# A Mamba-style cross-attention block: two bursts of ScalarE work split, three more GpSimd products, fillers in the head

## The reference

```python
# per batch of 4; DI = 512 channels, N = 16 states, 512 positions
xin = in_proj(ctx)                              # 256 -> 512
u   = silu(causal_conv4(xin) + conv_b)
dt_low, B, C = split(x_proj(u))                 # 16, 16, 16 rows
dt  = softplus(dt_proj(dt_low) + dt_b)
state = state * exp(dt * A) + (dt * u) * B      # along the positions, 16 states a channel
y   = sum_n(state * C) + D * u
y   = y * silu(layernorm(x).T)                  # the gate
x   = x + y.T
out = x + layernorm(x) @ sum_r(factors[r]) / sqrt(8) + bias
```

## Time and profile before

| | us |
|---|---|
| median of 3 runs | 483.63 (482.84 to 483.75) |
| the profiled execution's own time | 482.48 |
| its span | 480.7 |
| VectorE busy | 453.5 (94%) |
| TensorE busy | 432.1 (90%) |
| GpSimd busy | 420.6 (88%) |
| ScalarE busy | 344.7 (72%) |

### The profile page before, as it was taken

The page is one execution under the profiler, slowest core; times in us unless marked ns, Lnnn a source line. Parts: engine busy times, 40 slices in busy tenths (PEclk is TensorE's granted clock), DMA queues, the critical chain, the costliest instruction groups (busy, mean ns, idle before and its releaser), DMA issues.

```text
span 480.7 us, 4118 instructions
## 1 busy us (share of the span) xinstructions
PE 432.1 (90%) x1119; PEld 185.3 (39%) x1119; DVE 453.5 (94%) x327; ACT 344.7 (72%) x578; POOL 420.6 (88%) x223
## 2 busy tenths in 40 slices
PE   8799797999979868898989789899979999989996
PEld 5134343434434233333434244343434343344432
DVE  5797999989999999989999999999999899999996
ACT  4669574977659788796869977697879876654422
POOL 4369999998979899997999979797998958999972
PEclk9989999999999989999999999999999999999999
DMA  5799746438982000100694000000396000000002
GB/s 193 267 355 350 200 80 138 83 55 217 292 337 88 1 0 0 42 25 1 191 412 168 0 22 1 0 24 0 132 381 237 1 22 23 22 22 22 0 1 88
DMA packets 16847, 53.96 MB, mean 112 GB/s; under 512 B 1828, under 2 KB 2084, under 8 KB 15800
## 3 DMA queue, kind: packets, MB, share of 16 engines
q1 hardware_dynamic: 15384, 45.14, 25.9%
q0 software_dynamic: 1152, 8.39, 8.8%
q10 hardware_dynamic: 288, 0.18, 0.1%
HBM read 49.24 MB, written 4.46 MB: 112 GB/s over the span
## 4 chain that ended last, share of the span: by engine, by line
POOL 53%; issue 20%; DVE 11%; ACT 6%; PE 4%; DMA 4%; SPq 1%; POOLq 0%; DVEq 0%; ACTq 0%
POOL h L1093 40%; POOL h L1086 9%; DVE dA L946 7%; POOL dtu L1079 3%; DMA c_rep<-bc_scratch 2%; PE y L519 2%; DVE acc L920 2%; ACT dA L776 1%; DMA chan<-channel 1%; DVE h L952 1%; PE work L415 1%; POOL fsum L1123 1%; DVE h L946 1%; ACT gate L690 0%; SPq L331 0%
## 5 line engine op out<-in xcount | busy, mean ns | idle before, releaser
L1093 POOL TENSOR_TENSOR h<-b_rep,dtu 128x1024 f32<-128x1024 f32 x127 | 302.3, 2446 | 12.3 <-DMA b_rep<-bc_scratch 11.3
L519 PE MATMUL y<-h,ident 128*128 128x512 f32 x508 | 236.5, 602 | 34.9 <-DVE h L952 33.0
L946 DVE TENSOR_TENSOR_SCAN dA<-dA,h 128x1024 f32<-128x1024 f32 x97 | 221.8, 2287 | 11.6 <-ACT dA L776 11.1
L776 ACT ACTIVATE dA<-dt,a_neg 128x512 f32<-128x512 f32 x256 | 166.0, 681 | 92.9 <-DVE h L952 76.2
L519 PEld LDWEIGHTS y<-h,ident 128*128 128x128 f32 x508 | 92.8, 190 | 166.2 <-issue 103.7
L952 DVE TENSOR_TENSOR h<-dA,c_rep 128x1024 f32<-128x1024 f32 x96 | 117.1, 1220 | 2.4 <-DMA c_rep<-bc_scratch 0.3
L1086 POOL TENSOR_TENSOR h<-h,c_rep 128x1024 f32<-128x1024 f32 x31 | 74.5, 2403 | 22.3 <-DVE h L946 22.3
L946 DVE TENSOR_TENSOR_SCAN h<-dA,h 128x1024 f32<-128x1024 f32 x31 | 70.6, 2279 | 0.1
L403 PE MATMUL work<-ctx_sb,w_in 128*128 128x512 f32 x60 | 30.6, 644 | 0.3 <-DMA w_in<-w_inT 0.2
L507 PE MATMUL work<-fsum,xnT 128*128 128x512 f32 x64 | 28.8, 592 | 0.0
L920 DVE SCALAR_TENSOR_TENSOR acc<-work,chan,acc 128x511 f32<-128x511 f32 (+2 forms) x30 | 21.6, 731 | 1.3 <-ACT acc L655 1.2
(11 more groups left out here) (128 smaller groups left out, 375.3 us busy)
## 6 DMA issues: line engine op xcount, KB each, us to landing
b_rep<-bc_scratch SPq DMA_DIRECT2D x32, 512.0 KB, 9.7
c_rep<-bc_scratch SPq DMA_DIRECT2D x32, 512.0 KB, 9.3
fsum<-factors POOLq DMA_DIRECT2D x8, 1024.0 KB, 8.3
x<-x SPq DMA_DIRECT2D x4, 1024.0 KB, 7.7
out<-x SPq DMA_DIRECT2D x16, 256.0 KB, 2.0
ctx_sb<-ctxT SPq DMA_DIRECT2D x3, 512.0 KB, 5.7
ctx_sb<-ctxT SPq DMA_DIRECT2D x2, 256.0 KB, 4.4
w_in<-w_inT SPq DMA_DIRECT2D x1, 384.0 KB, 5.2
```

Source lines behind the costliest of these rows:

```text
L519: mm = pe.matmul(y[:], ident[:], h[:, (s * PAIRS + j) % H_RING, i, :], start=False, stop=(j == sum_order(s)[-1] and i == 1))
L776: act.activation(dA[:, j % 2, i, :], dt[:, k % 2, :], ACT.Exp, scale=a_neg[:, k, 2 * j + i:2 * j + i + 1]).then_inc(exp_done, 1)
L946: dve.tensor_tensor_scan(pair if on_pool(s * PAIRS + j) else decay, decay, pair, 0.0, ALU.mult, ALU.add).then_inc(scanned, 1)
L1093: pool.tensor_tensor(h[:, (s * PAIRS + j) % H_RING], b_rep[:, j], dtu[:, k % 2, :].unsqueeze(1).to_broadcast([P, 2, L]), ALU.mult).then_in ...
```

## The change

- `SOFTPLUS_SLOTS`: softplus goes from slot 2 to slot 0 in steps 4, 8 and 12.
- The gate burst is made in two halves of two blocks each, each with its own table loads: slots 4 and 6 in step 0, slots 2 and 5 in steps 4, 8 and 12. The first half waits for one gate product fewer.
- The silu burst is made in two parts: blocks 0 to 2 of the next batch in slot 4 where k is 1 (steps 1, 5, 9), block 3 in slot 4 where k is 2 (steps 2, 6, 10).
- `STATS_SLOTS`: the statistics are in slot 5 in steps 0 and 2, in slot 3 in all others.
- `POOL_C`: steps 3, 9 and 11 have one C product more on GpSimd (pair 2 in step 3, pair 4 in steps 9 and 11). With it the order of TensorE's sums changes in these steps.
- `FIRST_FILL`: 6, 0, 2 and 2 zero-weight matmuls of 128 x 512 (bf16) ahead of the four parts of the first `x_proj`, and 3 behind it, into a bank of dA that is not yet used.

```diff
--- before.py
+++ after.py
@@ -57,11 +57,14 @@
 TENSOR_CONV = (5, 6, 7, 8, 9)
 SUM_ORDERS = {(0,): (1, 0, 2, 3, 4, 5, 6, 7), (0, 2): (1, 0, 3, 2, 4, 5, 6, 7), (0, 2, 4): (1, 0, 3, 2, 5, 4, 6, 7),
               (0, 4): (1, 0, 2, 3, 5, 4, 6, 7)}
-POOL_C = ((0, 4), (0,), (0, 2), (0,), (0, 2), (0, 2), (0, 2), (0, 2, 4), (0, 2), (0, 2), (0, 2), (0, 2), (0, 2), (0, 2),
-          (0, 2), (0, 2))
-SOFTPLUS_SLOT = 2
+POOL_C = ((0, 4), (0,), (0, 2), (0, 2), (0, 2), (0, 2), (0, 2), (0, 2, 4), (0, 2), (0, 2, 4), (0, 2), (0, 2, 4), (0, 2),
+          (0, 2), (0, 2), (0, 2))
+SOFTPLUS_SLOTS = (2, 2, 2, 2, 0, 2, 2, 2, 0, 2, 2, 2, 0, 2, 2, 2)
+GATE_SLOTS = ((4, 6), (2, 5), (2, 5), (2, 5))
 C_LAG = 3
+STATS_SLOTS = (5, 3, 5, 3, 3, 3, 3, 3, 3, 3, 3, 3, 3, 3, 3, 3)
 TENSOR_RESIDUAL = (0, 1, 2, 6, 8)
+FIRST_FILL = (6, 0, 2, 2, 3)
 IDLE_FILL = {(0, -1): 14, (0, 3): 3, (1, 3): 4, (3, 3): 4, (4, 1): 3, (5, 6): 2, (7, 6): 2, (8, 1): 2, (8, 6): 2, (9, 6): 2,
              (10, 1): 4, (11, 1): 2, (12, 1): 3, (13, 1): 3, (14, 3): 3}
 
@@ -416,9 +419,15 @@
                                    stop=(i == TAPS - 1))
                 mm.then_inc(conv_mm, 1)
 
+            def fill_first(i):
+
+                for _ in range(FIRST_FILL[i]):
+                    pe.matmul(dA[:, 1, 1, :], still[:], ones[:], start=True, stop=True)
+
             def x_proj(b):
                 for k in range(KB):
                     if b == 0:
+                        fill_first(k)
                         pe.wait_ge(u_done, k + 1)
                     mm = pe.matmul(first_bc if b == 0 else work2[0:2 * N + BC_ROW, :], w_x[:, k, :], u[:, b % 2, k, :], start=(k == 0),
                                    stop=(k == KB - 1))
@@ -614,6 +623,7 @@
             pe.wait_ge(w_x_landed, 16)
             pe.wait_ge(pads_ready, 1)
             x_proj(0)
+            fill_first(KB)
             pe.wait_ge(w_dt_landed, 16)
             pe.wait_ge(conv, conv_count(KB - 1))
             pe.wait_ge(dtl_evac, 1)
@@ -673,20 +683,20 @@
                 act.wait_ge(conv, conv_count(k))
                 act.activation(u[:, 0, k, :], acc[:, k, :], ACT.Silu).then_inc(u_done, 1)
 
-            def silu_batch(b):
-
-                wait_conv(act, b * KB + KB - 1)
+            def silu_blocks(b, first, last):
+
+                wait_conv(act, b * KB + last - 1)
                 if b >= 2:
                     act.wait_ge(y_init, (b - 1) * KB)
                     act.wait_ge(d_dtu, (b - 1) * KB)
-                act.activation(u[:, b % 2], acc[:], ACT.Silu).then_inc(u_done, KB)
-
-            def gate_batch(b):
+                act.activation(u[:, b % 2, first:last], acc[:, first:last], ACT.Silu).then_inc(u_done, last - first)
+
+            def gate_half(b, half):
 
                 act.wait_ge(g_nb, (b + 1) * KB)
                 if b > 0:
-                    act.wait_ge(gated, b * KB)
-                for k in range(KB):
+                    act.wait_ge(gated, b * KB - 1 + half)
+                for k in range(half * (KB // 2), (half + 1) * (KB // 2)):
                     act.activation(gate[:, k, :], x1_block(b, k), ACT.Silu, bias=g_r[:, 2, k:k + 1],
                                    scale=g_r[:, 1, k:k + 1]).then_inc(g_done, 1)
 
@@ -801,7 +811,7 @@
                         act.wait_ge(f_centred, i + 1)
                         act.activation(fsum[:, i, :], fsum[:, i, :], ACT.Copy, scale=FR ** -0.5).then_inc(f_scaled, 1)
 
-                    if j == SOFTPLUS_SLOT and is_d:
+                    if j == SOFTPLUS_SLOTS[s] and is_d:
                         act.preload_act_table_set("softplus")
                         softplus(s + 1)
                         act.preload_act_table_set("natural_log_exp_and_others")
@@ -823,21 +833,21 @@
                         conv_out(KB + 1)
                     if j == 3 and s > 0 and s + KB + 1 in TENSOR_CONV:
                         conv_out(s + KB + 1)
-                    if j == (5 if k == 0 else 3) and is_g:
+                    if j == STATS_SLOTS[s] and is_g:
                         act.wait_ge(x_landed, (b + 2) * 16)
                         act.wait_ge(g_nb, (b + 1) * KB)
                         minus_mean(g_mv, b + 1, k, g_scratch, g_mean)
                     if j == 3 and s - 1 in TENSOR_RESIDUAL:
                         x1_evac(s - 1)
-                    if j == 4 and k == 0:
+                    if k == 0 and j in GATE_SLOTS[b]:
                         act.preload_act_table_set("silu_and_others")
-                        gate_batch(b)
+                        gate_half(b, GATE_SLOTS[b].index(j))
                         act.preload_act_table_set("natural_log_exp_and_others")
-                    if j == 4 and k == KB - 2 and b + 1 < BATCH:
+                    if j == 4 and k in (1, KB - 2) and b + 1 < BATCH:
                         act.preload_act_table_set("silu_and_others")
-                        silu_batch(b + 1)
+                        silu_blocks(b + 1, *((0, KB - 1) if k == 1 else (KB - 1, KB)))
                         act.preload_act_table_set("natural_log_exp_and_others")
-                    if j == (5 if k == 0 else 3) and is_g:
+                    if j == STATS_SLOTS[s] and is_g:
                         var_sum(g_mv, b + 1, k, g_scratch, g_mean, s + 1, g_var)
                     if j in (2 if s == STEPS - 1 else 4 if s == STEPS - 2 else 6 if s == STEPS - 3 else 5, 7):
                         for w in w_at(s)[j // 7:j // 7 + 1]:
```

## The result

| | before | changed |
|---|---|---|
| median, us | 483.63 (5 runs) | 480.31 (479.59 to 481.48, 5 runs) |
| ratio | | 0.9934 [0.9919, 0.9948] |
| the profiled execution, us | 482.48 | 481.48 |

What follows compares the result with a forecast made beforehand. Outside head and tail, VectorE's work plus ten waits for ScalarE's decay factors (11.1 us) bound the kernel. Step terms summed to -2.5, or -2.8 with some 0.1 more per removed wait: 483.63 to 480.8 us, range 478.5 to 483.8.

Steps and rivals of the forecast that it cites:

- the head: Stretch with the zero-weight filler matmuls: put at 0, with bounds of -0.8 and +0.9 us.
- The burst prices: ScalarE's bursts with table loads: gate half 4.07 us, silu of three blocks 4.1, of one block 3.2, softplus 3.2.
- step 9: Three-block silu burst plus third GpSimd product: VectorE waits 2.9 us, net +1.7 with the product's gain included.
- Product terms: Extra GpSimd C products, each taking 1.26 us off VectorE: -1.3 in step 3, nothing from those in steps 9 and 11.
- Step 12: Softplus early and gate in halves: VectorE waits 1.5 us at pair 1; -0.3 for steps 11 and 12 together.
- Step 4: Softplus in slot 0, gate halves in slots 2 and 5: +0.35 at pair 1, -0.2 us in all.
- step 0: Gate split over slots 4 and 6: 1.5 us gained at pair 5, later wait at pair 7, net +0.7.
- the C wait: VectorE's wait at 36.5 us for a C row from DRAM: to grow to about 1 us, its landing unmoved.
- ScalarE's loads: Rival: the added table loads, 18.0 us, are paid nearly in full as VectorE stalls; slower, up to 487.1 us; 8 in 100.
- The pause behind each load: Rival: a pause as long as a load follows each of 14 added loads, giving 498.7 us; 1 in 100.
- The third products: Rival: the extra GpSimd products bring nothing, step 3's failing too for lack of ScalarE slack: 482.1 us; 15 in 100.
- The head got no shorter: Rival: the head gets shorter by an earlier or varying C-row landing and faster clock: -0.8, 480.0 us; 12 in 100.

Runs made afterwards that it cites:

- the two repeats: The changed kernel run again twice without edits: medians 481.56 and 481.57 us, ratios 0.9952 and 0.9957 to the kernel before.
- third profile of the changed kernel: The changed kernel, unedited, in its second repeat: median 481.57 us, ratio 0.9957 to the kernel before.
- changed_again: The changed kernel, unedited, in its first repeat: median 481.56 us, ratio 0.9952 to the kernel before.
- gate0_whole: Against the changed kernel, step 0's gate burst whole in slot 4: median 480.21 us, ratio 0.9929 to the kernel before.
- whole_and_c1: Against the changed kernel, gates of steps 0 and 12 and silu of batches 1 and last whole, second GpSimd product in step 1: 476.72 us.
- c9_c11_back: Against the changed kernel, third GpSimd products of steps 9 and 11 back on VectorE: median 483.38 us, ratio 0.9984 to the kernel before.

## Why the prediction was right

The time fell inside the range, 0.5 us from the forecast in the first job and about as far on the other side in the two repeats (2.3 and 2.1 for 2.8). The mechanism is borne out step by step; how near the first median came is luck in part, since the head moves the time by as much.

**What bounds the kernel** was read rightly: the waits for ScalarE and VectorE's work. Every body step came out within 0.2 us of its term. The 0.1 that the sum added for each of the three removed waits did not come: the terms of the body add up to -3.9 without it, and it measured -3.8. **The burst prices** hold: 4.13 for 4.07, and in step 9 the parts are these:

```profile
287.71 1.29 ACT L786 ACTIVATE dA<-dt,a_neg 128x512 f32<-128x512 f32 x2
...
289.02 1.28 ACT L847 ACT_TABLE_LOAD   x1
...
290.32 1.49 ACT L692 ACTIVATE u<-acc 128x1536 f32<-128x1536 f32 x1
...
291.82 1.28 ACT L849 ACT_TABLE_LOAD   x1
...
293.61 1.29 ACT L786 ACTIVATE dA<-dt,a_neg 128x512 f32<-128x512 f32 x2
```

From load to the next decay pair's start 4.6 us with the evacuation, as reckoned (4.1 and 0.5). The scan waited 3.16 where 2.9 was forecast, and 2.90 and 2.89 in the two repeats. In the first profile ScalarE had waited 0.91 us for a late matmul shortly before, at 284.20, which also made the 0.53 of pair 3. **Product terms**: step 3 pays 1.2, steps 9 and 11 together 0.3, shown by taking them back. **Step 12**: 1.32 at pair 1 for 1.5, and 0.99 at pair 6, where the forecast's starts give 380.9 - (373.1 + 2 x 3.46) = 0.9. **Step 4** was forecast at -0.2 and is 0.0, the smallest term. **GpSimd** never became a bound in the body: VectorE's one wait for it there is 0.5 us, in step 13, as before, and GpSimd itself still waits some 1.7 us for a scan in step 10.

**The weak term is step 0 and the head.** The split there costs 0.9 in place of 0.7. The other 0.5 of step 0 is head: the scan of its pair 3 starts at 37.67 before and at 37.94 in the first and third profile of the changed kernel, though the first scan of all is 0.3 to 0.6 earlier. There the held operation of the sign change makes it late. The head was put at 0. This scan starts at 38.48 in `changed_again` and at 40.65 in `gate0_whole`, where VectorE waits for the C row (0.34 and 1.63 us), so a landing moves it by 0.5 to 2.7 us from one execution to the next. The profiled pair of executions differs by 1.0 and not by 3.3 because this execution, the slowest of its five, has 0.9 more in step 9 by the clock and starts pair 3 no earlier. What of head, clock and chance made 3.2, 2.3 and 2.1 us of one kernel in three jobs, the profiles do not say.

**The signs.** The waits came where they were named. VectorE fell by 2.3 us and not by 3.6, for the held operation. The clock was at 1.00 from 22 to 44 us in two of the three profiles of the changed kernel, but the C wait did not grow to 1 us: it is 0, 0.34 and 0. One sign of being wrong did come, the landing of that row moved; it was taken as fixed and varies from one execution to the next. And the upper end of the range is not its own sum: 480.8 + 1.3 + 0.9 is 483.0, not 483.8.

**The rivals.** ScalarE's loads were not paid nearly in full: 18.3 us more of busy time gave 2.2 us more of waits, with the removed ones set against them. The pause behind each load is not there: 39.37 + 1.28 = 40.65, and the gate starts at 40.67. The Trainium skill gives 2.66 us with its drain for a switch (ScalarE: Activation LUTs, What ACT_TABLE_LOAD costs); that is twice what these rows show. The rule of the Trainium skill to batch calls by set (ScalarE: Activation LUTs, Table sets: the hidden batching unit) came out right for three splits, though not by its price: the gate bursts of steps 0 and 12 and the silu burst of the last batch were 0.9, 1.0 and 1.2 us better whole. The other two silu bursts were not: whole, they make VectorE wait 1.01 us in step 2 and 1.12 in step 6, split 0.61 in step 1 and 0.95 in step 5. The third products did nothing in steps 9 and 11, as forecast, and paid in step 3. The head got no shorter.

The forecast took the change as one. Its own terms said that steps 0, 9 and 12 lose what others gain; with those parts taken out, and the product of step 1 added, 3.5 us (481.57 - 478.10) and 4.9 us (481.57 - 476.72) more are gained in the same job. So the gain of the change is not one of the splits, which lost 3.1 us in three places and won some 0.6 in two. Of the 2.28 us of wait removed in step 2, 1.27 went by moving the statistics behind the burst: with the silu whole there and the statistics moved, `whole_and_c1` waits 1.01. The other large gain is the second product of step 3, 1.2. The gate halves of steps 4 and 8 were not tried whole; against the kernel before these steps changed by 0.0 and -0.2.

## What to carry to other kernels

When a helper engine runs one item ahead through two buffers, a burst costs only what is over the window (two items' time less two of the helper's own operations); write down that window at each place before splitting a burst, because the split adds its overhead at both. Taking work off the bounding engine just ahead of such a burst brings nothing, since it closes the window. Move small operations that stand ahead of the burst first: here they took from the same window, and moving them added no table load. And where the whole time jitters by more than the change is worth, compare stretches between two fixed instructions of the profile, and look there for a late matmul at the lower clock before a difference is put down to the edit.

## What the runs showed of the hardware that was not expected

A VectorE `tensor_scalar` over 128 x 4 floats in SBUF took 0.17 us, or as long as a running GpSimd `tensor_tensor` still needed: 1.30 in the first profile, and 1.86 in `gate0_whole` (first fence VectorE, second GpSimd):

```profile
28.10 1.86 DVE L1015 TENSOR_SCALAR g_mv<-g_mv 128x4 f32<-128x4 f32 x1
```

```profile
27.55 2.38 POOL L1104 TENSOR_TENSOR h<-b_rep,dtu 128x1024 f32<-128x1024 f32 x1 [11.28 <-DMA b_rep<-bc_scratch]
```

28.10 + 1.86 = 29.96, 27.55 + 2.38 = 29.93. In `c9_c11_back` the operation at 28.45 took 0.17, and GpSimd's product began at 28.55. In the other profiles that have this operation it starts inside that product and ends within 0.05 us of it, except before the change, where the product was over and it took 0.17. The Trainium skill (SBUF — State Buffer, SBUF: two separate sides) describes a pair of ports that VectorE and GpSimd share as an exclusive lock: whichever starts first has it for its whole instruction, and the other blocks. The trace agrees for this operation. The scans and C products, which have one input in PSUM, keep their 2.29 and 1.22 beside running GpSimd products.

TensorE's clock fell in different places in profiles of the same kernel (steps 5 and 8 in the first, at 24 to 26 us and at the start of step 1 in the third), and cost time where a late matmul stood ahead of ScalarE's decays: 0.6 to 1.1 us in step 1 of four profiles, 0.9 and 1.2 in step 9, 1.8 in step 6. In the third profile it was back at 2.4 GHz before the matmuls of step 1 that ScalarE waits for, and nothing was lost.
